# Local transformer layers on one core: PSUM as one pool of eight banks placed over a pair of slots, rotation and norms one slot later, a new matmul order

## The reference

```python
# _L1_ffn_ref, DEPTH = 6, HEADS = 16, DIM_HEAD = 64, WINDOW = 32, INNER = 1024, DIM_INNER = 341
def attn_layer(x, Wqkv, qs, ksc, Wo):
    q, k, v = split_heads(x @ Wqkv)
    q = l2norm(q) * qs;  k = l2norm(k) * ksc
    q = q * cos * scale + rotate_half(q) * sin * scale
    k = k * cos / scale + rotate_half(k) * sin / scale
    # windows of 32 tokens; each sees its own window and the one before
    sim = einsum('bhwie,bhwje->bhwij', bq, look(bk)) * 8.0   # masked
    out = einsum('bhwij,bhwje->bhwie', softmax(sim), look(bv))
    return out @ Wo
def ffn_layer(x, g, bln, W1, b1, W2, b2):
    xn = (x - mean) / sqrt(var + 1e-05) * g + bln
    a, gate = split(xn @ W1 + b1)
    return a * gelu(gate) @ W2 + b2
for i in range(6):
    x = attn_layer(shift_tokens(x), ...) + x
    x = ffn_layer(shift_tokens(x), ...) + x
```

## Time and profile before

| | |
|---|---|
| median of three runs | 7357.33 us (7355.12 to 7366.33) |
| the profiled execution | 7357.27 us, its span (first to last instruction) 7355.0 us |
| instructions | 148821 |
| the local layers | from 3020 us to 7305 us of the span, 58% of it |
| busy share of the span | PE 74%, PEld 45%, DVE 57%, ACT 40%, POOL 36% |

### The profile page before, as it was taken

How to read it: one execution, slowest core, us unless ns; L and a number is a source line. 1 busy time by engine, 2 the same in 40 slices (tenths; PEclk the granted TensorE clock), 3 DMA queues, 4 the chain that set the end, 5 groups by cost and what they waited for, 6 DMA issues and landing times. The chain is left out here.

```text
span 7355.0 us, 148821 instructions
## 1 busy us (share of the span) xinstructions
PE 5433.0 (74%) x55030; PEld 3293.8 (45%) x55030; DVE 4220.0 (57%) x5698; ACT 2963.7 (40%) x4797; POOL 2646.5 (36%) x1392
## 2 busy tenths in 40 slices
PE   4727775295867859488888888888888888888885
PEld 3524443021222212255555555555555555555554
DVE  4352113241423233678777777777777777777775
ACT  0002222032222313355555555555555555555552
POOL 0000000000000000566556665665566666666662
PEclk8758888597887969799999999999999999999997
DMA  0000000301000010111111111111111111111111
GB/s 17 0 7 26 26 26 19 50 1 26 1 17 9 0 26 0 60 33 30 31 50 29 32 29 50 29 32 29 49 29 32 29 50 32 29 30 36 30 31 40
DMA packets 153434, 202.65 MB, mean 28 GB/s; under 512 B 40904, under 2 KB 79698, under 8 KB 151614
## 3 DMA queue, kind: packets, MB, share of 16 engines
q1 hardware_dynamic: 153312, 201.04, 12.0%
HBM read 63.67 MB, written 11.53 MB: 10 GB/s over the span
## 5 line engine op out<-in xcount | busy, mean ns | idle before, releaser
L1594 POOL TENSOR_TENSOR d_qk_swap<-d_qk_raw,d_rot 128x512 f32<-128x512 f32 x768 | 971.7, 1293 | 987.8 <-ACT d_qk_raw L1317 987.8
L1601 POOL TENSOR_TENSOR d_rnorm<-d_sq_clip,neg_half 128x32 f32<-128x32 f32 x192 | 1048.6, 5461 | 414.2 <-DVE d_sq_clip L1474 414.0
L99 POOL TENSOR_TENSOR ln_post_rstd<-ln_post_var,neg_half 128x8 f32<-128x8 f32 x16 | 26.9, 1683 | 2920.6 <-DVE ln_post_var L80 2920.6
L1154 PE MATMUL d_ring<-d_wqkv,d_xin 128*128 (+1 forms) x1536 | 795.9, 647 | 144.4 <-ACT d_qk_raw L1317 64.6
L866 DVE TENSOR_REDUCE c_mx<-c_ps 128x1 f32<-128x512 f32 (+3 forms) x768 | 417.1, 556 | 774.4 <-PE c_ps L737 770.6
L834 ACT ACTIVATE c_pt<-c_ps 128x512 f32<-128x512 f32 (+1 forms) x640 | 354.5, 555 | 1122.3 <-PE c_ps L752 1120.3
L1169 PE MATMUL d_ring<-ident,d_qk_part 128*128 128x128 f32 x3072 | 451.1, 288 | 278.8 <-ACT d_qk_raw L1317 168.8
L766 PE MATMUL c_ps<-c_pt,c_vg 128*32 128x512 f32 (+3 forms) x1536 | 632.2, 509 | 4.7 <-DVE c_ots L871 4.7
L1470 DVE TENSOR_REDUCE d_sq_sum<-d_qk_sq 128x32 f32<-128x2048 f32 x192 | 438.7, 2285 | 224.9 <-ACT d_qk_sq L1324 222.0
L1169 PEld LDWEIGHTS d_ring<-ident,d_qk_part 128*128 128x128 f32 x3072 | 349.1, 144 | 463.6 <-ACT d_qk_raw L1317 224.8
L1154 PEld LDWEIGHTS d_ring<-d_wqkv,d_xin 128*128 128x128 f32 x1536 | 293.4, 205 | 519.7 <-issue 407.4
(11 more groups left out here) (256 smaller groups left out, 9534.3 us busy)
## 6 DMA issues: line engine op xcount, KB each, us to landing
d_band<-d_own_t SPq DMA_DIRECT2D x768, 64.0 KB, 2.0
d_band<-d_prev_t SPq DMA_DIRECT2D x576, 64.0 KB, 2.0
d_v_prev<-d_v SPq DMA_DIRECT2D x191, 128.0 KB, 2.3
b_w<-in_L_ffn_w SPq DMA_DIRECT2D x64, 256.0 KB, 3.3
d_band_prev<-d_prev_t SPq DMA_DIRECT2D x192, 64.0 KB, 2.0
d_wqkv<-in_L_ffn_Wqkv SPq DMA_DIRECT2D x6, 1536.0 KB, 9.3
c_kp<-c_k_scratch SPq DMA_DIRECT2D x30, 256.0 KB
c_qp<-c_q_scratch SPq DMA_DIRECT2D x24, 256.0 KB
```

The costliest lines, as they stand in the source:

```text
L1154: eng.matmul(ring[c % 3][:, :], xin[p][:, :], wqkv[:, bass.ds(par, 1), c * 512:(c + 1) * 512].rearrange("p l n -> p (l n)"), start=True, s ...
L1594: mm = eng.tensor_tensor(qk_swap[:, which, :, out:out + hd], qk_raw[:, which, :, src:src + hd], rot[:, bass.ds(par, 1), which, 1, bass.ds( ...
L1601: eng.tensor_tensor(rnorm[:, :], sq_clip[:, :], neg_half[:, 0:2 * HEADS], ALU.pow).then_inc(rn_ready, 1)
```

## The change

The arithmetic is the same, instruction for instruction; only places in PSUM, waits and the order within a slot differ.

- **PSUM.** The eight banks are four pairs, `d_pair0` to `d_pair3`, and every product has a bank of its own by slot parity (`QK_AT`, `TURN_AT`, `V_AT`, `SP`, `W1_AT`, ...). The four qk products of a slot lie in four banks, the scores of even and odd slots in different ones.
- **DVE and POOL.** The addition of the rotation moves from slot n to the head of slot n+1, directly ahead of the multiplication by the norms (`rotated` holds both now). The two `cosine` halves are taken apart, the second behind `centred`. `blocks` of a tile moves from the head of slot n+3 to slot n+2, behind `total`; so POOL's multiplication of the probabilities comes ahead of `d_qk_swap` in odd slots and ahead of `d_rnorm` in even ones. The second residual moves from the odd slot to the next even one, which makes the pipeline one slot longer (`TILES + 7`).
- **SP.** The band's DMAs are issued behind the copy of `v_prev`, one slot earlier by tile, and the loads of the next layer's weights stand between slots 6 and 7 of a layer with a band transfer between them.
- **PE.** Even and odd slots have code of their own. W1's three groups are spread: one at the end of the even slot, two between the qk matmuls of the odd slot. The variance and W2 go ahead of the turns of the even slot, Wo between the turns of the odd slot.

```diff
-        ring = [... nc.psum_tensor(f"d_ring{k}", [P, 512], F32)) for k in range(3)]
-        sp = ctx.enter_context(nc.psum_tensor("d_sp", [P, 2, 8, 2 * WIN], F32))
-        op = ctx.enter_context(nc.psum_tensor("d_op", [P, 8, P], F32))
-        ff = ctx.enter_context(nc.psum_tensor("d_ff", [P, 2, FB], F32))
+        pair = [ctx.enter_context(nc.psum_tensor(f"d_pair{k}", [P, 2, 512], F32)) for k in range(4)]
+        QK_AT = ((2, 0, 3, 6), (6, 4, 5, 1))
+        TURN_AT = ((7, 0, 5, 4), (7, 6, 5, 7))
+        V_AT = ((2, 0), (1, 4))
+        SP = [pair[k][:].rearrange("p o (j c) -> p o j c", c=2 * WIN) for k in (2, 1)]
+        op = pair[3][:].rearrange("p a (c t) -> p (a c) t", t=P)
+        W1_AT = (0, 2, 3)
+        WO_AT, C_AT, VAR_AT, BC_AT, W2_AT = 4, 0, 4, 1, 1
...
+                    def even_slot():
+                        near, far = live(6), live(8)
+                        if f:
+                            eng.wait_ge(sub_ready, n - 1)
...
+                            qk(0)
+                            qk(1)
+                            qk(2)
+                        if live(4):
+                            eng.wait_ge(ot_ready, n - 3)
+                        if a:
+                            qk(3)
...
+                        if s:
+                            eng.wait_ge(rope_ready, n)
+                            turn(0)
+                            raw_read(0)
+                            values(0)
+                            raw_read(1)
+                            turn(1)
...
+                            turn(2)
...
+                            turn(3)
+                            turn_read(1)
+                            values(1)
+                            scores()
+                        if g:
+                            raw_read(3)
+                            attended()
...
                     def rotated():
-                        eng.wait_ge(cos_done, n + 1)
-                        eng.wait_ge(swap_ready, n + 1)
-                        flat = qk_part[p][:].rearrange("p a h d -> p (a h d)")
+
+                        eng.wait_ge(cos_done, n)
+                        eng.wait_ge(swap_ready, n)
+                        flat = qk_part[1 - p][:].rearrange("p a h d -> p (a h d)")
                         eng.tensor_tensor(flat, flat, qk_swap[:].rearrange("p a h d -> p (a h d)"), ALU.add)
                         eng.drain().then_inc(added, 1)
+                        eng.wait_ge(rn_ready, n)
+                        heads = qk_part[1 - p][:].rearrange("p a h d -> p (a h) d")
+                        eng.tensor_tensor(heads, heads, rnorm[:, :].unsqueeze(2).broadcast_to((P, 2 * HEADS, DH)),
+                                          ALU.mult).then_inc(rope_ready, 1)
...
@@ gpsimd
+                    if u == 1 and f:
+                        normalise()
                     if a:
                         par, i = eng.snap(parity(n)), eng.snap(n % TB)
                         if s:
                             eng.wait_ge(added, n)
...
+                    if u == 0 and f:
+                        normalise()
+                    if a:
                         eng.wait_ge(ss_ready, n + 1)
                         if s:
                             eng.wait_ge(rope_ready, n)
                         eng.tensor_tensor(rnorm[:, :], sq_clip[:, :], neg_half[:, 0:2 * HEADS], ALU.pow).then_inc(rn_ready, 1)
```

354 lines of the change are left out of this document (197 added, 157 removed).

## The result

The changed kernel takes **6681.4 us** (median of four runs, 6677.3 to 6685.4), against 7356.2 us for the kernel before on the same chip: a ratio of 0.908, 95% interval 0.9065 to 0.9097. The direction was right, the size was not: the prediction of 6820 us was 139 us too high, and 6681 lies just under its low end of 6710.

The account below looks back on a forecast made before the run. Bound: a loop through PE and DVE, closed by few PSUM banks and queue order. DVE's 36.07 + 1.3 + 0.2 + 0.4 + 0.2 gives 38.2 us a pair against 44.03; 7357 - 542 + 5 = 6820 us, range 6710 to 7020.

Parts of the forecast that it names:

- The bound before: Old pair of slots, 44.03 us: bound by a loop through PE and DVE, closed by few PSUM banks and queue order.
- The floor, 36.07: DVE's stretches of a pair without waits, gaps between its instructions included: 36.07 us, not removed by the change.
- The stall, 1.3: DVE waits 1.3 us a pair at the odd slot's block transposes for POOL's multiplication of the probabilities, which takes 2.52.
- The cosines apart, 0.2 a pair: Splitting the two cosines on DVE costs at most one more instruction start, set at 0.1 us a slot.
- Margins, 0.4: PE and POOL deliver to DVE early, three margins being 1 to 1.6 us; 0.4 us a pair added for margins used up.
- PE's holes: In the changed kernel PE's holes lie at the first turn of each slot, released by DVE's norm.
- Tables and layer starts: Rotation tables on DVE add 3.3 us a layer, 0.2 a pair; PE's 4.95 us wait for band DMAs at layer starts goes.
- The sum of a pair: Floor, stall, cosines and margins make 38.0 us for a plain pair; with the tables 38.2 against 44.03.
- The ends of the pipeline, +5 us: Emptying the pipeline over one more slot adds at most 5 us to the kernel.
- the floor alone: Rival: short stall and no margin used up, 36.3 + 0.2 us a pair, 6665 us; chance 0.09.
- POOL and DVE in each other's way: Rival: swap and power contend with DVE's cosines and additions every slot; 40.7 a pair, 7055 us; 0.19 shared with clock near L 10.
- The clock: Rival: small matmuls and waits lower PE's clock; at 22 us of a pair at 1.2 GHz, 7480 us; slower has chance 0.07.

Follow-up runs that it names:

- add_early: Changed kernel with the rotation's addition moved back to its own slot, behind both cosines and ahead of `centred`, only the norm staying at the next slot's head: 7313.2 us.
- pe_plus: Changed kernel with two of the four groups of transposes of each slot made twice on PE, 0.98 us more PE work a slot: 6789.1 us.
- sums_first: Changed kernel with DVE's row sums and their reciprocal put ahead of the addition and the norm in odd slots: 7104.1 us.

## Why the prediction was right and where it was wrong

- **The bound before: right as far as tested.** Waits for banks put back into the changed kernel cost 233 us, so they were a part of the loop through PE and DVE. That the order of DVE's queue closed it too is argued: `add_early` (+632) closes another loop, over `centred` and the shared banks, which the kernel before did not have. That this one place in DVE's order can cost nearly all of the gain was not in the prediction: it treated the late addition as a way to hide the swap, and priced the cosines apart at 0.1 us a slot as pure cost. Measured, the cosine behind `centred` is worth 203 us, as cover for PE.
- **The floor, 36.07: too high by 0.57.** In a pair of 36.27 us, less the wait of 0.77, the same instructions with their gaps take 35.50. Before, the gaps without a releaser were 2.0 us of a pair; now 1.5. The prediction had taken them along as fixed. The term that failed is the gaps, not the work: DVE's busy time a pair is 33.4 us (33.3 before).
- **The stall, 1.3: right in place and releaser, measured 0.78.** The step that failed is POOL's 2.52 us. That row stood beside DVE's two-input addition. In its new place the multiplication has only row-wise and PSUM-reading instructions beside it and takes 1.90 us.
- **The cosines apart, 0.2 a pair: nothing that shows.** The one behind `centred` follows it without a gap, and the 35.50 hold all four.
- **Margins, 0.4:** DVE waits for scores nowhere and for Wo once, so none was used up, though `pe_plus` shows that Wo had less than 0.5 us. What took the term's place is `sq_clip` and `xn` held by POOL: (303 - 180) x 2 + (693 - 410) ns are 0.5 us a pair. That the number is near is luck.
- **PE's holes:** the one at the first turn of the odd slot came as predicted. The one at the first turn of the even slot did not, but for a few pairs: there are 104 waits for the norm in 93 pairs.
- **Tables and layer starts:** the five pairs with tables are 2.6 to 4.6 us above their neighbours, on both sides of the 3.3 of the prediction; the four instructions take 2.49 us, and the longer ones also change the phase of POOL and DVE. PE's wait for the band's DMA has gone as predicted. The three starts of 40.2 to 40.8 us are 3.5 to 4.1 too long: PE stands up to 4.4 us ahead of its qk products, put down to `issue`, and DVE 4.4 to 5.0 us for the variance behind them. The second and the last layer start without it. The kernel before has the same hole at the same three starts (3.5 to 3.9 us), so the change neither made it nor took it away; the prediction did not see it, and its cause stays open.
- **The sum of a pair:** 0.57 of the floor, 0.52 of the stall and 0.2 of the cosines were too much, together 1.3; 0.1 for the layer starts was missing, and the pairs other than those of 36.27 have 0.5 where the margins had 0.4. This is the 1.15 us between 38.2 and 37.05, and 93 x 1.15 = 107 of the 139 us. The mechanism was the right one with its terms mis-sized, most of them towards the high end. The prediction's account of the old pair also closes 0.2 us too long (42.6 against 42.4).
- **The ends of the pipeline, +5 us: measured -22.** This is the other 27 of the 139 us (the rest is the profiled execution against the median). The slot more that the pipeline takes to empty costs less than the emptying pairs save: the last two before the end take 25.6 and 22.5 us, before 35.4 and 32.2. With 37.05 a pair the prediction's own sum gives 7357 - 649 + 5 = 6713 us, inside its range, and it is this term that puts the time below the low end of 6710. The prediction priced the additional slot and put the saving at nothing without a reason. The rival "the floor alone" (6665 us) came nearest, with 36.5 a pair and the same +5; its 16 us are two errors that cancel in part.
- **POOL and DVE in each other's way:** right as a danger; the changed kernel misses it where the prediction said, as norm and swap are held apart and the swap takes 4.96 us. Its price of 40.7 a pair and 7055 us is near the 7104 of `sums_first`, but by luck: that kernel pays for one norm held by 1.5 us a pair, for row sums 1.5 us ahead of it and for a wait of 4.0 behind PE at a low clock, not for 1.0 us in each slot. And the prediction looked only at two-input instructions. The Trainium skill (SBUF — State Buffer, Who interferes with whom) lists `tensor_scalar` among those that can contend in a two-port mode, and says that whoever issues first has the shared ports for the whole instruction while the other is blocked. The rows agree with such blocking: `sq_clip` went from 0.18 us to 0.66 to 1.95, each time with its end at an end of POOL. Its form with two SBUF inputs did so too. In which mode `sq_clip` runs no row shows.
- **The clock:** it rose to 1.00 instead of falling. PE's busy time fell from 36.0 to 34.2 us a pair, the 34.3 that the prediction gave for full clock.

Is DVE's queue the bound now? Mostly: DVE is idle for another engine only 1.0 us a pair, and added DVE work costs its full time and more. But as I read it the loop over PE and ACT is within 0.5 us of it: every way of sparing DVE up to 2 us gained at most 0.5 us a pair. Neither filling the stall nor freeing the held instructions alone gives a gain of their own size.
